# A fused attention kernel in full precision: rounded products for the last values, packed row terms, small diagonals on POOL, new order tables

## What is computed

```python
# layer 0: linear attention over 32 + 32 heads of 8 channels
qkv = [x@wq.T, x@wk.T, x@wv.T]                     # 768 channels
pw  = conv1x1_grouped(dwconv5x5(qkv))              # 768 more
scores = einsum('bhdn,bhen->bhde', [value, 1], relu(key))
out    = einsum('bhde,bhen->bhdn', scores, relu(query))
x1     = bn(conv1x1(out[:-1] / (out[-1:] + 1e-15))) + x
# layer 1: full attention over the 1024 positions
norm   = (x1 - mean(x1)) / sqrt(var(x1) + 1e-5)    # per channel
F, G   = f_w@norm + f_b, g_w@norm + g_b
H      = h_w@x1 + h_b
result = o_w @ (H @ softmax(F.T @ G, axis=-1).T) + o_b + x1
```

## Time and profile before

| what | value |
|---|---|
| runs (median; lowest to highest) | 678.85 us; 677.8 to 681.25 us, 3 runs |
| the profiled execution | 678.21 us, of which span 676.4 us |
| mean granted clock of PE | 0.985 of 2.4 GHz |
| batch 0's first `pwkv` transposes | 85.4 us; batch 1: 243.0; batch 2: 396.3; batch 3: 556.7 |
| attention loop of the last batch | from 616.1 us |

### The profile page before, as it was taken

One profiled execution on the slowest core, in us unless ns is written; L12 is line 12 of the kernel. 1 busy time (PEld: TensorE's weight loads), 2 busy tenths in 40 slices (PEclk: granted clock), 3 DMA queues, 4 the chain that ended last, 5 costly groups with the idle time before them and its releaser, 6 DMA issues.

```text
span 676.4 us, 13121 instructions
## 1 busy us (share of the span) xinstructions
PE 631.8 (93%) x5456; PEld 461.4 (68%) x5456; DVE 523.8 (77%) x603; ACT 469.8 (69%) x764; POOL 487.3 (72%) x229
## 2 busy tenths in 40 slices
PE   5988999999899999999999999997979999899998
PEld 3854465647688866647778866646758875478887
DVE  4999995878887799768889999989899995363321
ACT  4797497966768889968686869875756876233331
POOL 4799749399889999949999979877996996010000
PEclk9899999999899999999899999998989999999999
DMA  8000000101100000001100000000100000000000
GB/s 309 9 1 4 3 1 2 63 1 63 62 1 32 17 16 2 1 1 63 63 0 16 32 2 17 2 2 0 63 0 17 16 17 17 1 1 0 16 17 31
DMA packets 6698, 16.67 MB, mean 25 GB/s; under 512 B 880, under 2 KB 1136, under 8 KB 6128
## 3 DMA queue, kind: packets, MB, share of 16 engines
q1 hardware_dynamic: 6640, 15.84, 6.6%
HBM read 11.64 MB, written 4.19 MB: 23 GB/s over the span
## 4 chain that ended last, share of the span: by engine, by line
PE 71%; DVE 10%; issue 7%; ACT 7%; POOL 2%; DMA 1%; SPq 0%; DVEq 0%; POOLq 0%; ACTq 0%
PE ps L767 12%; PE ps L743 10%; PE ps L578 7%; PE ps L846 5%; PE ps L512 4%; PE ps L516 3%; PE ps L513 3%; PE ps L758 3%; DVE ps L1317 3%; PE ps L778 2%; PE ps L812 2%; ACT prod L1032 2%; POOL conv L1580 2%; PE ps L586 2%; PE ps L893 2%
## 5 line engine op out<-in xcount | busy, mean ns | idle before, releaser
L1580 POOL TENSOR_TENSOR conv<-conv,prod 128x930 f32<-128x930 f32 (+4 forms) x174 | 382.8, 2239 | 59.8 <-ACT prod L1032 57.1
L1317 DVE SCALAR_TENSOR_TENSOR ps<-raw,dw_sb,ps 128x930 f32<-128x930 f32 (+4 forms) x264 | 317.0, 1201 | 6.8
L1032 ACT ACTIVATE prod<-raw,dw_sb 128x961 f32<-128x961 f32 (+4 forms) x209 | 217.1, 1101 | 1.2 <-POOL conv L1580 1.2
L767 PE MATMUL ps<-ht,pt 128*128 128x256 f32 x512 | 115.1, 379 | 0.0
L767 PEld LDWEIGHTS ps<-ht,pt 128*128 128x128 f32 x512 | 95.1, 190 | 11.8
L1210 ACT ACTIVATE rows<-ps,small 128x1024 f32<-128x1024 f32 x32 | 35.7, 1115 | 74.5 <-DVE small L1510 74.5
L1580 POOL TENSOR_TENSOR rows<-rows,prod 128x930 f32<-128x930 f32 (+4 forms) x26 | 58.2, 2240 | 17.1 <-ACT prod L1032 13.6
L1505 DVE TENSOR_REDUCE small<-ps 128x1 f32<-128x1024 f32 x32 | 39.1, 1223 | 28.4 <-PE ps L743 28.4
L743 PE MATMUL ps<-hi,t_hi 128*128 128x512 f32 x128 | 46.8, 448 | 7.0 <-ACT rows L1210 7.0
L743 PE MATMUL ps<-lo,t_hi 128*128 128x512 f32 x128 | 41.7, 407 | 0.0
L512 PE MATMUL ps<-hi,wqkv_hi 128*128 128x512 f32 x92 | 37.8, 411 | 2.3 <-ACT t_sums L1063 1.5
(11 more groups left out here) (172 smaller groups left out, 1069.2 us busy)
## 6 DMA issues: line engine op xcount, KB each, us to landing
q_raw<-x_dram SPq DMA_DIRECT2D x8, 512.0 KB, 5.5
x<-x_dram SPq DMA_DIRECT2D x4, 1024.0 KB, 4.7
out_dram<-x_t SPq DMA_DIRECT2D x16, 256.0 KB, 2.0
conv<-wqkv_dram SPq DMA_DIRECT2D x1, 768.0 KB, 4.3
conv<-fg_dram SPq DMA_DIRECT2D x1, 512.0 KB, 6.0
proj_sb<-proj_dram SPq DMA_DIRECT2D x1, 512.0 KB, 7.5
pw_sb<-pw_dram SPq DMA_DIRECT2D x1, 384.0 KB, 6.7
mask_sb<-masks_dram SPq DMA_DIRECT2D x1, 280.0 KB, 6.4
```

What stands on the lines that cost most here:

```text
L767: mm = pe.matmul(dst[:, 0:C], pt[:, i % PT_BUFS, j, :], ht[:, j, :], start=(j == 0), stop=(j == NB - 1))
L1032: act.activation(dst, view, ACT.Copy, scale=weight(t, i)).then_inc(prod_ready, 1)
L1317: return dve.scalar_tensor_tensor(dst, view, w, before, ALU.mult, ALU.add)
L1580: pool.tensor_tensor(total, total, product, ALU.add).then_inc(conv_pool, 1)
```

## The change

1. **Values of the last batch** (`last_values` for `values` in batch 3). ACT rounds the transposed probabilities as it takes them from PSUM (`last_pt_hi`), DVE subtracts to get the rest (`last_pt_lo`) and frees the bank (`t_free`, before ACT's). ACT rounds `ht` behind each `t_hi` (`last_ht_hi`), POOL subtracts (`last_ht_lo`). PE does high by high, high by low and low by high: 24 rounded matmuls of 256 columns for eight in full precision. The four arrays lie over the images `raw`, which the last batch no longer needs.
2. **Row terms.** Eight matmuls in four column groups (32x256: `rstd_v` broadcast to 32 columns as weights, a quarter of `x1` streaming) behind unit 0; ACT copies them to `s_masked` ahead of its `t_hi` of unit 1; PE transposes two blocks behind unit 2; ACT picks one column of 32 per quarter ahead of its `t_hi` of unit 3.
3. **Fold spread** once instead of twice: two matmuls; DVE multiplies both halves of `fg` by the same spread half, the second half first.
4. **Small diagonals** for the batches 1 to 3 come from POOL, behind both `rstd` and a wait for the projection.
5. **Tables** set anew, some twenty-five of them; `ROWS_AT` is gone. `RSTD_AT` from ((12, 13), (13, 14), (16, 16)) to ((14, 15), (15, 15), (16, 16)); `FIRST_SPLIT` from 13 to 24.

```diff
-PRODUCTS_T = ((0, 2, 4, 0), (2, 0, 0, 1), (1, 0, 0, 2))
-ROWS_AT = (3, 3, 2, 0)
+PRODUCTS_T = ((0, 2, 1, 1), (1, 0, 2, 0), (1, 0, 1, 2))
...
+            def last_values(b, i):
+                pe.wait_ge(t_free, 16 * b + 2 * (i + 1))
+                if i == 0:
+                    pe.wait_ge(last_ht_lo_ready, D_HT)
+                dst = d_slot(D_AT["v", b] + i)
+                for j in range(NB):
+                    high, low = last_weights(last_pt_hi, i)[:, j, :], last_weights(last_pt_lo, i)[:, j, :]
+                    pe.matmul(dst[:, 0:C], high, last_ht_hi[:, j, :], start=(j == 0), stop=False)
+                    pe.matmul(dst[:, 0:C], high, last_ht_lo[:, j, :], start=False, stop=False)
+                    mm = pe.matmul(dst[:, 0:C], low, last_ht_hi[:, j, :], start=False, stop=(j == NB - 1))
+                mm.then_inc(d_full, 1)
...
                 for c in range(CK):
-                    for k in range(CK):
-                        mm = pe.matmul(dst[:, k * C + c * P:k * C + (c + 1) * P],
-                                       stat_rstd[:, c:c + 1].to_broadcast([P, P]), ident, start=True, stop=True)
+                    mm = pe.matmul(dst[:, c * P:(c + 1) * P], stat_rstd[:, c:c + 1].to_broadcast([P, P]), ident,
+                                   start=True, stop=True)
...
-                    for i in range(blocks, blocks + ROWS_AT[u]):
+                    if u == 0:
                         for k in range(CK):
-                            mm = pe.matmul(terms[:, i:i + 1], x1[:, k, i * P:(i + 1) * P], rstd_v[:, k:k + 1],
-                                           start=(k == 0), stop=(k == CK - 1))
-                        if i == NB - 1:
-                            mm.then_inc(a_full, 1)
-                    blocks += ROWS_AT[u]
+                            for g in range(QUARTERS):
+                                mm = pe.matmul(terms[HEADS * g:HEADS * (g + 1), 0:QUARTER],
+                                               rstd_v[:, k:k + 1].to_broadcast([P, HEADS]),
+                                               x1[:, k, g * QUARTER:(g + 1) * QUARTER],
+                                               start=(k == 0), stop=(k == CK - 1))
+                        mm.then_inc(row_sums_full, 1)
+                    if u == D_T - 2:
+                        pe.wait_ge(row_sums_copied, b + 1)
+                        for j in range(CK):
+                            mm = pe.transpose(terms[:, QUARTER + j * P:QUARTER + (j + 1) * P], s_masked[:, j, :], ident)
+                        mm.then_inc(a_full, 1)
...
+                    if u == 1:
+                        act.wait_ge(row_sums_full, b + 1)
+                        act.copy(s_masked[:], terms[:, 0:QUARTER].rearrange("p (j q) -> p j q", j=CK)).then_inc(
+                            row_sums_copied, 1)
...
+                    if not with_next:
+                        act.wait_ge(d_free, ht_slot(b, u) + 1)
+                        act.copy(last_ht_hi[:, 2 * u:2 * u + 2, :], ht[:, 2 * u:2 * u + 2, :]).then_inc(last_ht_hi_ready, 1)
...
+                        if not with_next:
+                            act.copy(last_half(last_pt_hi, i, u), ps[:, T_PAIR + u, :]).then_inc(last_pt_hi_ready, 1)
+                            continue
...
-                if with_next:
-                    quad_products(later_weights, SHARED_TILE, QUAD_OF[b + 1]).then_inc(quad_weights_ready, 1)
...
-                for k in range(CK):
-                    op = dve.scalar_tensor_tensor(folded[:, k, :], fg[:, k, :], stat_rstd[:, k:k + 1], folded[:, k, :],
+                for k in reversed(range(CK)):
+                    op = dve.scalar_tensor_tensor(folded[:, k, :], fg[:, k, :], stat_rstd[:, k:k + 1], folded[:, 0, :],
...
+                    if 1 <= i <= NB and not with_next:
+                        for u in range(2):
+                            dve.wait_ge(last_pt_hi_ready, 2 * (i - 1) + u + 1)
+                            dve.tensor_tensor(last_half(last_pt_lo, i - 1, u), ps[:, T_PAIR + u, :],
+                                              last_half(last_pt_hi, i - 1, u).bitcast(F32),
+                                              ALU.subtract).then_inc(t_free, 1)
...
                 if b + 1 < B:
+                    pool.wait_ge(d_full, D_AT["proj", b] + D_PROJ)
+                    quad_products(pool, later_weights, SHARED_TILE, QUAD_OF[b + 1]).then_inc(quad_weights_ready, 1)
                     conv_adds(b + 1, RSTD_AT[b][1], ALL_TAPS)
...
+            for u in range(D_HT):
+                pool.wait_ge(last_ht_hi_ready, u + 1)
+                pool.tensor_tensor(last_ht_lo[:, 2 * u:2 * u + 2, :], ht[:, 2 * u:2 * u + 2, :],
+                                   last_ht_hi[:, 2 * u:2 * u + 2, :].bitcast(F32),
+                                   ALU.subtract).then_inc(last_ht_lo_ready, 1)
```

More of the change, by code:

```diff
@@ L173 @@
+FIRST_SPLIT = 24
+FIRST_WEIGHTS = 17
+FIRST_PRODUCTS_RAWKV = (0, 0, 0, 5, 0, 0, 0, 0)
+FIRST_PRODUCTS_KVT = (0, 2, 1, 1, 0, 0, 0, 1, 0)
+FIRST_PRODUCTS_RAWQ = (0, 0, 0, 1)
+FIRST_PRODUCTS_CONV = (3, 6, 1, 2, 0, 1)
 A_BANKS = 4
@@ L202, in conv_seq_kernel @@
         t_sums = nc.alloc_sbuf_tensor_at("t_sums", [P, 2, CK * N], F32, offset=sums_at)
+        images_at = nc.sbuf_base
         raw = sb("raw", [P, TILES, IMG])
+        last_ht_hi, last_ht_lo, last_pt_hi, last_pt_lo = (
+            nc.alloc_sbuf_tensor_at(name, [P, NB, C], F32R, offset=images_at + 4 * NB * C * n)
+            for n, name in enumerate(("last_ht_hi", "last_ht_lo", "last_pt_hi", "last_pt_lo")))
         conv = sb("conv", [P, TILES, N])
@@ L912, in body @@
                     p_transposes(b, i - 1)
-                    values(b, i - 2)
+                    (values if with_next else last_values)(b, i - 2)
                 p_transposes(b, NB - 1)
-                values(b, NB - 2)
-                values(b, NB - 1)
+                (values if with_next else last_values)(b, NB - 2)
+                (values if with_next else last_values)(b, NB - 1)
                 pe.wait_ge(t_free, 16 * (b + 1))
@@ L1194, in body @@
                 act.wait_ge(t_bias_ready, b + 1)
+                terms = a_bank(A_AT["row", b])
                 for u, (c, h) in enumerate(UNITS):
+                    if u == 1:
+                        act.wait_ge(row_sums_full, b + 1)
+                        act.copy(s_masked[:], terms[:, 0:QUARTER].rearrange("p (j q) -> p j q", j=CK)).then_inc(
+                            row_sums_copied, 1)
                     if u == D_T - 1:
                         act.wait_ge(a_full, A_AT["row", b] + 1)
[L1198 to L1199 removed]
+                        act.activation(row_c.rearrange("p (g j) -> p g j", j=CK),
+                                       terms[:, QUARTER:].rearrange("p (j g s) -> p g j s", g=QUARTERS, s=HEADS)[:, :, :, 0],
+                                       ACT.Identity, bias=row_k).then_inc(a_free, 1)
                     act.wait_ge(d_full, D_AT["t", b] + u + 1)
```

82 lines of the change are left out of this document (41 added, 41 removed).

## The result

The changed kernel takes 659.56 us (median of four runs, 658.94 to 660.01) against 680.03 us (677.8 to 681.25) of the kernel before in the same job: a ratio of 0.9731, 95% interval 0.968 to 0.9783. The forecast was 660 us. The profiled execution has a span of 657.6 us against 676.4, 18.8 us less.

The account below looks back on a forecast made before the run. PE's queue was taken as the bound, provided POOL, DVE and ACT are not late with the next batch's convolution. Terms summed to 18.3 us off 678.2, giving 659.9; with 0.6 for the median, put at 660 us, range 652 to 671.

Parts of the forecast that it names:

- Values (4.6 - 0.7 us): Last batch's attention loop: 24 rounded matmuls at 0.12 us save 4.6 us; later `t_free` and the loop's start cost 0.7.
- in sequence: Rival, last batch's values: weight load and stream add up to 0.220 us a record; 679 us, no change; chance 0.05.
- full-precision rate: Rival, last batch's values: 256 rounded columns take 0.43 us a matmul; 720 us, slower; chance 0.03.
- Fold spread (1.9 us): PE's fold spread in each batch: half of eight records go, 0.49 us per batch, 1.9 us in all.
- Row terms (8.6 us): PE's transformed units: one-column matmuls replaced by eight matmuls and two transposes, 2.15 us less per batch, 8.6 in four.
- I price the wait at nothing: Row terms: the two transposes' wait for ACT's copy of 256 columns costs nothing, since a whole unit (1.49 us) lies between.
- the table term of 1.0 us: Batch 0, fourth `t_hi` and spreads: two and one products ahead instead of four, 1.0 us gained on PE.
- Small diagonals (6.4 us): Batch 2: moving DVE's product to POOL ends PE's waiting and slow clock, 6.4 us; POOL's product taken as 1.0 us.
- the stall: Batch 2: PE waits 4.61 us for `ht` behind DVE's 6.78 us product, then loses 0.93 and 0.88 us to slow clock.
- Tables and feeders (+1.0 - 3.5 us): New tables gain 1.0 us in batch 0; late feeders take back 1.5, 0.5 and 1.5 us in batches 0 to 2.
- the feeders hold: Rival: POOL, or DVE and ACT, is late, so PE's gains in batches 0 to 2 are partly lost; 669 us; chance 0.20.

Follow-up runs that it names:

- the filling: Changed kernel with idle gaps of PE filled by transposes of the unit matrix and matmuls adding zero, batches 0 to 3: 653.61 us, ratio 0.9673.

## Why the prediction was right, and where it was not

- **Values (4.6 - 0.7 us).** Right in every part: 0.12 us a record, a period of 6.50 us, and the loop from its first energy to the end 60.26 - 56.58 = 3.68 us shorter against 3.9. The price between 0.105 and 0.231 us was chosen by the transposes, and they were the right neighbour: loads of 128 columns (0.105 us) and streams of 256 alternate every 0.12 us, so loads hide. By the Trainium skill (TensorE: Matmul & The Clock Gate, "Back-to-back issue gap") it would have been 109 ns; the trace says 120. The rivals "in sequence" (0.22), with the rule named for it, and "full-precision rate" (0.43) fell.
- **Fold spread (1.9 us).** 0.97 us became 458.96 - 458.43 = 0.53 us, 0.44 a batch against 0.49.
- **Row terms (8.6 us).** On PE the size was right: 9.34 - 7.41 = 1.93 us in the last batch, where nothing else stands in ACT's and DVE's queues, against 2.15. The step that failed is "I price the wait at nothing" together with the table term of 1.0 us: in batches 0 to 2 the units are held by two other queues, and alone the edit brought nothing (ratio 1.0019), or some 3 of the 8.6 us with the low clock taken out. I had named ACT's products as a condition and DVE's four taps not at all. Row terms and tables are one edit there; together the way from the first unit to the spreads fell by 2.89, 1.79 and 1.39 us in the three batches.
- **Small diagonals (6.4 us).** The mechanism was right: the stall and its slow clock are gone, and POOL needs 0.83 us against the 1.0 taken. The size was read from one execution, whose 6.78 us product was the longest of the twelve that DVE made in four executions; eight of them took 1.70 to 2.70 us, and three 0.55. That the three in the earlier trace rows differ more than tenfold under the same code was in the rows, and was the sign that the largest was no typical one. The typical worth is 2.8 to 3.8 us in the old tables and 5.6 in the new, in part clock in both.
- **Tables and feeders (+1.0 - 3.5 us).** The sign was wrong. Taken together nothing was given back in batches 0 to 2 (16.6 us gained against the 15.3 of the terms without the 3.5), and without the new tables some 11 us of the result are missing. The rival "the feeders hold" describes the code with the old tables (a ratio of 0.989 where its 669 us over 678.85 made 0.985); it does not describe the change, because the tables are what lifts it. Each product or tap has to leave one place and be on time at another, and I counted only the first.
- **What hit the sum.** The stretches of low clock, 10.1 us in the profile of before ((1 - 0.985) x 676.4) and 6.6 in that of after, are 3.5 us of the 18.8, of which I had counted 1.8 behind the stall. In batch 1 the kernel before had one at 334 us (1.7 us), the changed kernel none; in batch 3 the changed kernel has one in the projection (8.71 against 7.11 us) and the kernel before none. The rest of batch 3's longer front is 1.5 us ahead of the projection's second half: PE's 96 small matmuls took 4.72 us in place of 4.01, their weight loads waited 1.2 us for ACT's copies of `vt` against 0.5, and one late product more stands in ACT's queue. So that the total came out right to 0.5 us was luck, two errors against each other: batches 0 to 2 gained 4.8 us more than forecast, and the start, batch 3's front and its units 4.4 us less. (The sum itself gives 659.9 + 0.6 = 660.5 us, put down as 660.)

## What to carry over

A matmul removed from the critical engine is worth its time only if every queue that feeds the next wait can come earlier too; read each of them (here ACT's products, and behind them DVE's taps) before counting it, and count a new order together with the work that needs it. A stall in a single profile is a sample: look at the same instruction in the other batches, and in another execution where there is one, before pricing it. And where PE must wait for a microsecond anyway, fill the wait with harmless matmuls: it cost nothing here and gave back 0.8%. Two kernels whose clocks differ by 0.005 differ by 3 us for that alone, so compare the clocks before the times.

## What the hardware did unexpectedly

- PE's granted clock fell to 0.50 (1.2 GHz) for 3.4 us or twice that (0.58 over four microseconds is 3.4 us at 0.50, and 0.57 over eight is 6.9), four times in the profile of the changed kernel and five times in that of the kernel before, and cost 1.7 us or twice that each time. In the changed kernel the falls followed waits of PE (1.13 us ahead of 178.46, 1.48 ahead of 574.09), but not the same ones each time: behind the wait of 1.38 us ahead of 328.70 the clock stayed at 1.00, and in the second execution of the same kernel, behind the same wait of 1.38 us, it was 0.76 over the next 7 us. That the waits bring these falls is shown by the filling: with four of them filled the mean clock was 0.997 in all six runs. Which of the waits is followed by a fall stays open, and so does the fall at 30.2 us of the second execution, which no wait precedes. The scatter of the kernel before is mostly this: its runs at a mean clock of 0.989 and above took 671.5 to 675.4 us, those at 0.982 and below 676.5 to 681.6.
- A short DVE product with all its data in SBUF can be held by POOL's adds, and past several adds in a row: 7.01 us for a product that takes 0.35. The others were held to the end of one add (0.55 to 2.70 us), and the reciprocal of `den` never was (1.75 us, eight times in an execution). The Trainium skill (SBUF — State Buffer, "SBUF: two separate sides") gives DVE's operations with two SBUF inputs, and its two-port modes, a port pair that it shares with GpSimd and that is locked for an instruction. The runs agree for two SBUF inputs, and the product by a scalar was held too (that it runs in such a mode, no run shows); they go beyond it in one point: twice DVE did not get its turn between two adds (7.01 and 6.78 us).
